# Softmax row sums partly added by accumulating DMAs, summed in a bank of the scores, and normalised on GpSimd

## The chip, the cores and the metric

One core of a Trainium2 chip runs one program. The metric is the device time of that program in microseconds (us), as the median of several runs. TensorE multiplies matrices, ScalarE applies functions such as the exponential, VectorE and GpSimd work on elements, SyncE issues most of the DMAs. SBUF holds 128 partitions of data; PSUM holds eight banks of 128 x 512 float32, into which TensorE writes.

## The reference, cut to what matters

The program computes attention with 32 heads of width 32 over 2 batches of 2048 rows, a gate made from a linear layer with a routed low-rank part, and their product added to the input.

```
xn     = layernorm(x)                                   # x: 2 x 2048 x 1024
q,k,v  = xn @ wq, xn @ wk, xn @ wv                      # 32 query heads, 8 key/value heads, width 32
scores = q k^T * 32**-0.5, causal mask
attn   = softmax(scores)                                # exp(s - shift) / row sum
s      = (attn @ v) @ wo
g      = silu(xn @ W_base.T + b + routed low-rank part)
out    = x + s * g
```

The change lies in the softmax: the sum of exp over the keys of each query row, and the division by it.

## The kernel before

The program has four parts, one after the other: `project` (layer norm, transposes, q, k, v and the low-rank part), `attend`, `gate` and `output`. The change is in `attend`, which works on 16 groups (2 batches x 8 key/value heads); each group has 4 query heads that share k and v.

Within a group the 2048 query rows are 4 chunks of 512 (c = 0 to 3). Chunk c needs key tiles j = 0 to 4c+3, of 128 keys each. For a pair of key tile j and query tile i, one matmul (L898) gives the scores of all four heads with the keys on the partitions, in one of 3 banks `cols_ps`; for tiles on the diagonal a second matmul (L901) adds the mask. ScalarE takes the exponential (L942) into `probs`, 5 buffers of 128 x 2048 that each hold one key tile j for the whole chunk. A group has 136 such tiles (10, 26, 42 and 58 by chunk), 2176 in all. The shift in the exponent comes from row maxima that are made ahead for the chunks to come: row scores (L818) into 3 banks `rows_ps`, then a maximum on VectorE (L963, or L967 with a mask). 84 of these row pieces are made before the group's first tile, and from there on about 1.2 per tile, so TensorE always alternates between L898 and L818.

The order of the work is written out by hand. `stage(c)` lists the operations: "T" a score tile, "S" a row piece, "M" the turning of the shifts, "W" the weighing of two key tiles, and the events of a finished chunk. All engines walk the same list and each carries out its own kinds, so an operation's place in the list sets what is queued behind it on its engine. `event(t, ...)` places an operation after tile t of the group.

"W" (function `weigh`) multiplies v with two `probs` tiles into `o_ps` (L856, four heads side by side; the trace has two records for each matmul, so 16 for two tiles). The row sums lie in their own bank `l_ps`: matmuls with a matrix of ones. Of the key tiles in `ADDS[c]` (L595: 0, 5, 8 and 11 of the tiles of the chunks) GpSimd makes one tile `added` (L801, one instruction for each but the first), and one set of matmuls sums that (L870); each other key tile has matmuls of its own (L863), in the same "W" as its L856.

When a chunk is done, "O" copies `l_ps` and `o_ps` to SBUF on ScalarE (L952, L953), and SyncE moves the sums: "L1" (L763) gathers them into a small tile, VectorE takes the reciprocal ("I", L1010), "L2" and "L3" (L767, L771) store it and spread it over the partitions, and "N" multiplies the chunk by it on VectorE (L1014, two inputs of 128 x 512 in SBUF). "L4" stores the chunk. The events stand 2, 4, 8, 9, 13, 18 and 19 tiles behind the chunk's last "W".

ScalarE writes key tile j into a buffer of `probs` only when the tile that was in it is weighed, and added where GpSimd adds it (L936 to L941).

```
1013:  dve.wait_ge(l_spread[cc % 2], n.lin(32 * NREP, 16 * NREP * (cc // 2 + 1) - 32 * NREP * back))
1014:  nc.vector.tensor_mul(o_sb[cc % 2][:, :], o_sb[cc % 2][:, :], l_all[cc % 2][:, :]).then_inc(norm_ready, 1)
```

Of the kernel before, what the change touches and what calls it, by code (L numbers as in the profile page):

```python
# [28 lines left out]
P = 128  # L29
B, S, D = 2, 2048, 1024  # L30
T = B * S
# [467 lines left out]
NROWS, NCOLS, NPROBS = 3, 3, 5  # L499
# [19 lines left out]
assert NJG % NPROBS == 0  # L519
# [7 lines left out]
def cols_slot(t):  # L527
    return 1 if t == NTG - 1 else t % NCOLS
# [16 lines left out]

EVENTS = {}
# [18 lines left out]

# [28 lines left out]

ADDS = [[], [0, 1, 2, 4, 5], [0, 1, 2, 4, 5, 6, 8, 9], [0, 1, 2, 4, 5, 6, 8, 9, 10, 12, 13]]  # L595
NADD = sum(len(a) - 1 for a in ADDS if a)


def adds_through(c, j):

    return sum(max(0, len(a) - 1) for a in ADDS[:c]) + sum(1 for t in ADDS[c][1:] if t <= j)


def attend(nc, sc, ident, ident_r, mask_ji, tri, wb, lb, gw_hi, gw_lo):

    ctx = ExitStack()
    with ctx:
# [13 lines left out]
        added = sb("added", [P, NREP, CH])  # L621
        row_max = [sb(f"row_max{i}", [P, NREP, TPC, CPB]) for i in range(2)]
# [7 lines left out]
        l_all = [sb(f"l_all{i}", [P, CH]) for i in range(2)]  # L630
        gw_raw = sb("gw_raw", [P, 2, D])
# [3 lines left out]
        l_ps = ctx.enter_context(nc.psum_tensor("l_ps", [P, CH], FP32))  # L635

        passed = sem("a_passed")
        passed_rows = sem("a_passed_rows")
        q_loaded = [sem(f"a_q_loaded{i}") for i in range(CPB)]
# [11 lines left out]
        sum_done = sem("a_sum_done")  # L651
# [36 lines left out]
        def probs_of(c, j):  # L688
            return probs[(J_OFF[c] + j) % NPROBS]
# [18 lines left out]
        def _(sp):  # L708
# [30 lines left out]
            def run(n, c, ops):  # L739
                last_group = isinstance(n.pair, int) and n.lin(1) == NG - 1  # L740
                for op in ops:
                    kind = op[0]
                    if kind == "T" and op[2:] == (0, 0):

                        if c > 0 or not isinstance(n.pair, int) or n.pair > 0 or n.u > 0:
                            wait_apart(sp, probs_ready, n.lin(NTG, T_OFF[c]), passed)
# [7 lines left out]
                    elif kind == "M":  # L754
                        move_row(rows_count(n, op[1], op[2]), op[4])
                    elif kind in ("L1", "L2", "L3", "L4"):
                        cc, back = op[1:3]
                        par = cc % 2
                        count = n.lin(CPB, cc + 1 - CPB * back)
                        few = sc["l_inv"][par].rearrange("h (x f) -> (h x) f", f=NL)  # L760
                        if kind == "L1":
                            wait_apart(sp, chunk_copied, count, passed)
                            sp.dma_start(l_few[par][:, :], l_sb[par][0:P:HD, :].rearrange("h (x f) -> h x f", f=NL)) \  # L763
                              .then_inc(l_moved[par], 16)
                        elif kind == "L2":
                            wait_apart(sp, l_inv_ready, count, passed)
                            sp.dma_start(few, l_inv[par][:, :]).then_inc(l_inv_stored, 16)  # L767
                        elif kind == "L3":
                            wait_apart(sp, l_inv_stored, n.lin(16 * CPB, 16 * (cc + 1 - CPB * back)), passed)
                            for h in range(NREP):  # L770
                                sp.dma_start(l_all[par][h * HD:(h + 1) * HD, :], sc["l_inv"][par, h, :].partition_broadcast(HD)) \  # L771
# [11 lines left out]
        def _(pool):  # L783
# [28 lines left out]
        def _(pe):  # L812
# [14 lines left out]
            pe.sem_inc(rows_full, 1)  # L827
            pe.wait_ge(ones_ready, 1)
# [12 lines left out]
            def weigh(n, cc, back, j0):  # L841

                steps = TPC * (cc + 1)
                to_sum = [j for j in range(steps) if j not in ADDS[cc]]
# [7 lines left out]
                pe.wait_ge(probs_ready, n.lin(NTG, tiles_through(cc, j0 + 1) - back * NTG))  # L852
# [6 lines left out]
                for j in (j0, j0 + 1):  # L859
                    q0 = max(0, j - TPC * cc) * P  # L860
                    if j in to_sum:
                        for h in range(NREP):
                            ins = nc.tensor.matmul(l_ps[h * HD:(h + 1) * HD, q0:CH], ones[:, :],  # L863
                                                   probs_of(cc, j)[:, h, q0:CH], start=(j == to_sum[0]),
                                                   stop=(j == to_sum[-1] and not ADDS[cc]), tile_position=(0, h * HD))
                ins.then_inc(values_done, 1)
                if j0 == steps - 2 and ADDS[cc]:
                    pe.wait_ge(pool_added, n.lin(NADD, adds_through(cc, NJG) - back * NADD))
                    for h in range(NREP):
                        ins = nc.tensor.matmul(l_ps[h * HD:(h + 1) * HD, :], ones[:, :], added[:, h, :],  # L870
                                               start=False, stop=True, tile_position=(0, h * HD))
                    ins.then_inc(sum_done, 1)

            def run(n, c, ops):
                for op in ops:
# [12 lines left out]
                    elif kind == "T":  # L888
# [14 lines left out]
                    elif kind == "W":  # L903
                        weigh(n, *op[1:])
            over_stages(pe, run)

        @block.scalar
        def _(act):
            def load_gw(k):
# [14 lines left out]
            def run(n, c, ops):  # L924
                first_group = isinstance(n.pair, int) and n.pair == 0 and n.u == 0
                for op in ops:
                    kind = op[0]
                    if kind == "T":
                        t, j, i = op[1:]
                        act.wait_ge(cols_full, n.lin(NTG, t + 1))  # L930
                        if i == max(0, j - TPC * c):

                            g = J_OFF[c] + j - NPROBS
                            back = 1 if g < 0 else 0
                            if not (back and first_group):
                                act.wait_ge(values_done, n.lin(NVG, g // 2 + 1))  # L936
                                c5 = CPB - 1 if back else max(cc for cc in range(CPB) if J_OFF[cc] <= g)
                                j5 = g + back * NJG - J_OFF[c5]
                                if j5 in ADDS[c5]:
                                    act.wait_ge(pool_added, n.lin(NADD, max(adds_through(c5, j5), adds_through(c5, ADDS[c5][1]))  # L940
                                                                  - back * NADD))  # L941
# [15 lines left out]
        def _(dve):  # L957
# [37 lines left out]
            def run(n, c, ops):  # L995
                for op in ops:
# [270 lines left out]
def program(nc, x, wall, wo, wb, b_base, lb, out):  # L1267
# [14 lines left out]
    with ExitStack() as ctx:  # L1282
        ident = ctx.enter_context(nc.sbuf_tensor("ident", [P, P], FP32))
        tri = ctx.enter_context(nc.sbuf_tensor("tri", [P, CH], FP32))
        plain_ji = ctx.enter_context(nc.sbuf_tensor("plain_ji", [P, NREP, P], FP32))
# [4 lines left out]
        with nc.Block() as block:  # L1290
# [51 lines left out]
```

## Time and profile before

| | |
|---|---|
| median of 3 runs | 3931.12 us (3921.78 to 3934.61) |
| the profiled execution's own time | 3927.28 us |
| its span, first to last instruction | 3925.5 us |
| mean granted TensorE clock | 0.938 |
| busy: TensorE 91%, VectorE 54%, GpSimd 39%, ScalarE 37% | of the span |

The attention part takes the stretch from about 735 to 3150 us. PE is a matmul and PEld a weight load of TensorE, DVE is VectorE, ACT ScalarE, POOL GpSimd, SPq SyncE's queue. A line number such as L898 is a line of the kernel before. PEclk is the clock that TensorE was granted, as a share of 2.4 GHz.

### The profile page before, as it was taken

Reading aid. Unit: us, or ns where it says so; the run is one execution under the profiler, and the core shown is the slowest. Engines: PE = TensorE matmul, PEld = TensorE weight load, DVE = VectorE, ACT = ScalarE, POOL = GpSimd, SP = SyncE. Lnnn points to the kernel's source line nnn. Section 1 sums busy time; section 2 is a strip of 40 time slices with the busy share of each in tenths; the row PEclk is TensorE's granted clock in tenths of the full one; section 3 lists DMA queues with packets and bytes.
Section 4 is the critical chain, followed back from the end, with each engine's and each line's share of the span. In section 5 each row is a group of like instructions: output and inputs, shape, how many; then the busy total and the mean of one; then the engine's idle time right before and its main releaser. Section 6 shows DMA issues by size and latency. Waiting matters only on the chain. (4 is left out here: it accounts for less than half of the span.)

```text
span 3925.5 us, 62611 instructions
## 1 busy us (share of the span) xinstructions
PE 3565.3 (91%) x19072; PEld 2261.0 (58%) x19072; DVE 2117.8 (54%) x4677; ACT 1466.8 (37%) x2658; POOL 1526.7 (39%) x366
## 2 busy tenths in 40 slices
PE   7999998998988888888988989888888879998999
PEld 6888886444444444444444444444444368887887
DVE  5333323766666666666667667666767322222333
ACT  3122111454555454554545545544545511110000
POOL 0000000566565575665665665655756700000000
PEclk9999998798998998998989999988999989999999
DMA  6555554211111102112112112112020044444555
GB/s 215 171 167 161 156 158 128 74 45 36 51 43 38 50 22 59 47 27 53 50 32 53 42 37 53 36 44 51 20 60 26 12 154 150 140 140 149 193 193 176
DMA packets 262851, 344.52 MB, mean 88 GB/s; under 512 B 38560, under 2 KB 154272, under 8 KB 261024
## 3 DMA queue, kind: packets, MB, share of 16 engines
q1 hardware_dynamic: 258960, 328.32, 27.8%
q10 hardware_dynamic: 3600, 12.58, 0.9%
q8 instruction: 150, 2.46, 0.3%
q14 instruction: 141, 1.16, 0.1%
HBM read 205.03 MB, written 134.74 MB: 87 GB/s over the span
## 5 line engine op out<-in xcount | busy, mean ns | idle before, releaser
L942 ACT ACTIVATE probs<-cols_ps 128x512 f32<-128x512 f32 x2176 | 1180.1, 607 | 1191.9 <-PE cols_ps L898 1075.4
L801 POOL TENSOR_TENSOR added<-added,probs 128x2048 f32<-128x2048 f32 (+1 forms) x288 | 1282.2, 4452 | 374.6 <-ACT probs L942 359.2
L818 PE MATMUL rows_ps<-k_st,q_st 96*128 96x512 f32 (+3 forms) x2560 | 1015.2, 419 | 247.1 <-DVE row_max L963 163.4
L963 DVE TENSOR_REDUCE row_max<-rows_ps 128x1 f32<-128x512 f32 x1536 | 1007.3, 685 | 415.8 <-PE rows_ps L818 411.3
L898 PE MATMUL cols_ps<-q_st,k_st 97*128 97x512 f32 x2176 | 943.8, 442 | 23.7 <-ACT probs L942 11.9
L818 PEld LDWEIGHTS rows_ps<-k_st,q_st 96*128 96x128 f32 x2560 | 515.8, 202 | 538.0 <-DVE row_max L963 343.3
L967 DVE CUSTOM_DVE_ANT_0 masked_rows<-rows_ps,tri 128x128 bf16<-128x128 f32 (+3 forms) x1024 | 488.4, 484 | 319.3 <-PE rows_ps L818 316.6
L898 PEld LDWEIGHTS cols_ps<-q_st,k_st 97*128 97x128 f32 x2176 | 431.3, 199 | 379.0 <-issue 258.2
L856 PE MATMUL o_ps<-probs,v_st 128*32 128x512 f32 (+3 forms) x5120 | 588.4, 581 | 1.1 <-ACT probs L942 1.1
L801 POOL TENSOR_TENSOR added<-probs 128x2048 f32<-128x2048 f32 x48 | 219.8, 4578 | 554.0 <-ACT probs L942 554.0
L856 PEld LDWEIGHTS o_ps<-probs,v_st 128*32 128x32 f32 x5120 | 142.4, 117 | 316.5 <-issue 252.7
L786 POOL TENSOR_TENSOR gw_lo<-gw_raw,gw_hi 128x1024 fp32r<-128x1024 f32 x9 | 21.2, 2360 | 687.6 <-ACT gw_hi L919 687.6
L438 PE MATMUL acc<-xt_hi,w_hi 128*128 128x512 f32 x704 | 281.6, 400 | 0.4 <-DVE logits L381 0.4
L440 PE MATMUL acc<-xt_hi,w_lo 128*128 128x512 f32 x704 | 277.6, 394 | 0.0
L439 PE MATMUL acc<-xt_lo,w_hi 128*128 128x512 f32 x704 | 276.8, 393 | 0.0
L1140 PE MATMUL g_acc<-gw_hi,g_t_hi 128*128 128x512 f32 x576 | 224.8, 390 | 19.7 <-DMA g_t_lo<-scratch_hw_lo 19.7
L395 DVE SCALAR_TENSOR_TENSOR out_lo<-acc,out_hi 128x512 fp32r<-128x512 f32 x80 | 55.3, 691 | 324.3 <-ACT out_hi L290 324.3
L1014 DVE TENSOR_TENSOR o_sb<-o_sb,l_all 128x512 f32<-128x512 f32 x64 | 221.8, 3466 | 10.9 <-DMA l_all<-scratch_l_inv 10.9
L1142 PE MATMUL g_acc<-gw_hi,g_t_lo 128*128 128x512 f32 x576 | 224.6, 390 | 0.0
L1141 PE MATMUL g_acc<-gw_lo,g_t_hi 128*128 128x512 f32 x576 | 224.5, 390 | 0.0
L1260 PE MATMUL o_acc<-ow_hi,o_t_hi 128*128 128x512 f32 x512 | 200.3, 391 | 11.2 <-DVE o_t_lo L1226 11.2
L1261 PE MATMUL o_acc<-ow_lo,o_t_hi 128*128 128x512 f32 x512 | 199.9, 391 | 0.0
(101 smaller groups left out, 3032.8 us busy)
## 6 DMA issues: line engine op xcount, KB each, us to landing
q_st<-scratch_q_hi SPq DMA_DIRECT2D x128, 256.0 KB, 4.5
x_sb<-in_x SPq DMA_DIRECT2D x32, 512.0 KB, 4.1
scratch_xt_hi<-xt_hi SPq DMA_DIRECT2D x32, 512.0 KB, 6.0
scratch_xt_lo<-xt_lo SPq DMA_DIRECT2D x32, 512.0 KB, 6.8
scratch_q_hi<-out_hi SPq DMA_DIRECT2D x64, 256.0 KB, 2.4
scratch_q_lo<-out_lo SPq DMA_DIRECT2D x64, 256.0 KB, 2.9
q_st<-scratch_q_lo SPq DMA_DIRECT2D x64, 256.0 KB, 4.6
l_all<-scratch_l_inv SPq DMA_DIRECT2D x256, 64.0 KB, 2.0
```

The source lines that it names most:

```text
L438: nc.tensor.matmul(out, lh, rh, start=(k == 0), stop=False)
L439: nc.tensor.matmul(out, lh, rl, start=False, stop=False)
L440: ins = nc.tensor.matmul(out, ll, rh, start=False, stop=(k == KT - 1))
L801: nc.gpsimd.tensor_tensor(added[:, :, q0:CH], other[:, :, q0:CH], probs_of(c, j)[:, :, q0:CH], ALU.add).then_inc(pool_added, 1)
L818: nc.tensor.matmul(rows_ps[rows_slot(k)][:, 0:keys], q_st[c][0:K1, h, i * P:(i + 1) * P], k_st[kbuf][0:K1, CH * p:CH * p + keys], start=Tr ...
L856: ins = nc.tensor.matmul(o_ps[h * HD:(h + 1) * HD, q0:CH], v_st[vbuf][:, j, :], probs_of(cc, j)[:, h, q0:CH], start=(j == 0), stop=(j == s ...
L898: ins = nc.tensor.matmul(into, k_st[n.u][:, j * P:(j + 1) * P], q_st[c][:, :, i * P:(i + 1) * P], start=True, stop=not diagonal)
L942: nc.scalar.activation(probs_of(c, j)[:, :, i * P:(i + 1) * P], cols_ps[cols_slot(t)][:, :].rearrange("p (h q) -> p h q", h=NREP), ACT.Exp) \
L963: nc.vector.tensor_reduce(into, bank[:, :], AX.X, ALU.max).then_inc(rows_free, 1)
L967: nc.vector.tensor_tensor_reduce(masked_rows[rows_slot(k)][:, 0:keys], bank[:, 0:keys], tri[:, CH - keys:CH], 1.0, MASKED, ALU.add, ALU.ma ...
L1140: nc.tensor.matmul(acc[half][:, :], t_hi[u][:, k, :], w_hi[:, k, cols], start=(k == 0), stop=False)
L1142: ins = nc.tensor.matmul(acc[half][:, :], t_lo[u][:, k, :], w_hi[:, k, cols], start=False, stop=(k == NW - 1))
```

## The change

Six key tiles fit instead of five (`NPROBS` 6), the row scores have four banks instead of three (`NROWS` 4), and the bank `l_ps` is gone. Of the key tiles of chunks 1 to 3, GpSimd adds 4, 6 and 9 (`ADDS`; 3, 5 and 8 instructions), and DMAs issued from GpSimd's queue add 2, 4 and 5 (`DMA_ADDS`): the first is a copy into `dma_added`, the others are SBUF to SBUF with accumulation. A new operation "Y" (`row_sums`) comes right behind the chunk's last "W": it sums `added`, `dma_added` and the key tiles that are left (two for chunks 1 to 3, four for chunk 0) with matmuls into one of the 3 banks `cols_ps`, which takes its turn among the score tiles. Before "Y" TensorE waits for the GpSimd adds and the DMA adds of the chunk. ScalarE copies that bank to SBUF before its next tile. GpSimd's operations are now placed in the list as events "A" (add), "D" (DMA add) and "N". "N" runs on GpSimd. The events I, L2, L3, N, L4 stand 11, 12, 15, 19 and 20 tiles behind. The buffer for the gate's weights shares memory with the sixth `probs` buffer.

```diff
-NROWS, NCOLS, NPROBS = 3, 3, 5
+NROWS, NCOLS, NPROBS = 4, 3, 6
+ADDS = [[], [0, 1, 2, 4], [0, 1, 3, 4, 6, 8], [0, 1, 3, 4, 6, 7, 9, 10, 12]]
+DMA_ADDS = [[], [3, 5], [2, 5, 7, 9], [2, 5, 8, 11, 13]]
+REST = [[j for j in range(TPC * (c + 1)) if j not in ADDS[c] + DMA_ADDS[c]] for c in range(CPB)]
+    event(_t, "Y", _c)
     event(_t + 2, "O", _c)
     event(_t + 4, "L1", _c)
-    event(_t + 8, "I", _c)
-    event(_t + 9, "L2", _c)
-    event(_t + 13, "L3", _c)
-    event(_t + 18, "N", _c)
-    event(_t + 19, "L4", _c)
+    event(_t + 11, "I", _c)
+    event(_t + 12, "L2", _c)
+    event(_t + 15, "L3", _c)
+    event(_t + 19, "N", _c)
+    event(_t + 20, "L4", _c)
+    for _j in ADDS[_c][1:]:
+        event(tiles_through(_c, _j) - 1, "A", _c, _j)
+    for _j in DMA_ADDS[_c]:
+        event(tiles_through(_c, _j) - 1, "D", _c, _j)
...
+            def dma_add(n, c, back, j):
+                q0 = max(0, j - TPC * c) * P
+                wait_apart(pool, probs_ready, n.lin(NUG, used_through(c, j)), passed_pool)
+                if j == DMA_ADDS[c][0]:
+                    if sum_before(n, c) is not None:
+                        wait_apart(pool, cols_full, sum_before(n, c), passed_pool)
+                    pool.dma_start(dma_added[:, :, :], probs_of(c, j)[:, :, :]).then_inc(dma_done, 16)
+                else:
+                    wait_apart(pool, dma_done, n.lin(16 * NDMA, 16 * (dma_adds_through(c, j) - 1)), passed_pool)
+                    pool.dma_start(dma_added[:, :, q0:CH], probs_of(c, j)[:, :, q0:CH], accum_op=ALU.add).then_inc(dma_done, 16)
...
+                    elif op[0] == "N":
+                        _, cc, back = op
+                        wait_apart(pool, chunk_copied, n.lin(CPB, cc + 1 - CPB * back), passed_pool)
+                        wait_apart(pool, l_spread[cc % 2], n.lin(32 * NREP, 16 * NREP * (cc // 2 + 1) - 32 * NREP * back), passed_pool)
+                        nc.gpsimd.tensor_tensor(o_sb[cc % 2][:, :], o_sb[cc % 2][:, :], l_sb[cc % 2][:, :], ALU.mult) \
+                            .then_inc(norm_ready, 1)
...
-                for j in (j0, j0 + 1):
-                    q0 = max(0, j - TPC * cc) * P
-                    if j in to_sum:
-                        for h in range(NREP):
-                            ins = nc.tensor.matmul(l_ps[h * HD:(h + 1) * HD, q0:CH], ones[:, :],
...
+            def row_sums(n, cc, back):
+
+                bank = cols_ps[cols_slot(AT_Y[cc])]
+                pe.wait_ge(probs_ready, cols_free_count(n, AT_Y[cc]))
+                parts = [(probs_of(cc, j), max(0, j - TPC * cc) * P) for j in REST[cc]]
+                if ADDS[cc]:
+                    pe.wait_ge(pool_added, n.lin(NADD, adds_through(cc, NJG) - back * NADD))
+                    pe.wait_ge(dma_done, n.lin(16 * NDMA, 16 * (dma_adds_through(cc, NJG) - back * NDMA)))
+                    parts = [(added, 0), (dma_added, 0)] + parts
...
+                    elif kind == "Y":
+                        cc, back = op[1:3]
+                        act.wait_ge(cols_full, cols_count(n, AT_Y[cc]))
+                        act.wait_ge(o_stored[cc % 2], n.lin(32, 16 * (cc // 2) + 16 - 32 * back))
+                        nc.scalar.activation(l_sb[cc % 2][:, :], cols_ps[cols_slot(AT_Y[cc])][:, :], ACT.Copy) \
+                            .then_inc(probs_ready, 1)
...
-                    elif kind == "N":
-                        cc, back = op[1:3]
-                        dve.wait_ge(l_spread[cc % 2], n.lin(32 * NREP, 16 * NREP * (cc // 2 + 1) - 32 * NREP * back))
-                        nc.vector.tensor_mul(o_sb[cc % 2][:, :], o_sb[cc % 2][:, :], l_all[cc % 2][:, :]).then_inc(norm_ready, 1)
```

## Rows read from the trace of the kernel before

**Rows 1.** Windows view: the three parts of the program; per engine busy us (instructions).

```profile
core 0: us, PE busy (x) PEld busy (x) DVE busy (x) ACT busy (x) POOL busy (x), PEclk, DMA share, GB/s
0.00:735.00 735.00, 687.57 (x3422) 563.28 (x3423) 290.83 (x708) 164.28 (x277) 29.72 (x32) 0.95 0.52 162
735.00:3150.00 2415.00, 2133.88 (x12387) 1082.69 (x12386) 1602.80 (x3673) 1220.50 (x2278) 1496.99 (x335) 0.92 0.16 41
3150.00:3926.00 776.00, 743.88 (x3264) 615.03 (x3264) 224.21 (x298) 81.99 (x104) 0.00 (x0) 0.98 0.49 164
```

**Rows 2.** Groups by line, 735 to 3150 us: busy us, mean ns | idle before.

```profile
L801 POOL TENSOR_TENSOR added<-added,probs 128x2048 f32<-128x2048 f32 (+1 forms) x288 | 1282.2, 4452 | 374.6 <-ACT probs L942 359.2
...
L818 PE MATMUL rows_ps<-k_st,q_st 96*128 96x512 f32 (+3 forms) x2451 | 962.5, 411 | 228.9 <-DVE row_max L963 163.2 <-DVE row_max L967 62.0
...
L1014 DVE TENSOR_TENSOR o_sb<-o_sb,l_all 128x512 f32<-128x512 f32 x63 | 221.2, 3510 | 5.9 <-DMA l_all<-scratch_l_inv 5.9
...
L870 PE MATMUL l_ps<-added,ones 128*32 128x512 f32 x384 | 54.8, 618 | 16.1 <-POOL added L801 16.0
```

**Rows 3.** Timeline around one "N": VectorE, TensorE and GpSimd (start, us).

```profile
1507.47 4.06 DVE L1014 TENSOR_TENSOR o_sb<-o_sb,l_all 128x512 f32<-128x512 f32 x1
1511.46 1.27 DVE L963 TENSOR_REDUCE row_max<-rows_ps 128x1 f32<-128x512 f32 x2
...
1507.94 0.28 PE L818 MATMUL rows_ps<-k_st,q_st 96*128 96x256 f32 x1
1512.19 0.79 PE L818 MATMUL rows_ps<-k_st,q_st 96*128 96x512 f32 x1 [3.97 <-DVE row_max L963]
...
1506.44 8.40 POOL L801 TENSOR_TENSOR added<-added,probs 128x2048 f32<-128x2048 f32 x2 [6.26 <-ACT probs L942]
```

**Rows 4.** Timeline, TensorE: the stalls at the other three "N" of a group.

```profile
1543.52 0.80 PE L818 MATMUL rows_ps<-k_st,q_st 96*128 96x512 f32 x1 [4.13 <-DVE row_max L963]
...
1588.65 0.60 PE L818 MATMUL rows_ps<-k_st,q_st 96*128 96x512 f32 x1 [3.86 <-DVE row_max L967]
...
1648.11 1.10 PE L818 MATMUL rows_ps<-k_st,q_st 96*128 96x512 f32 x2 [1.29 <-DVE row_max L963]
```

**Rows 5.** Timeline: the last "N" of the kernel, with GpSimd idle, and the store.

```profile
3155.07 0.69 DVE L1014 TENSOR_TENSOR o_sb<-o_sb,l_all 128x512 f32<-128x512 f32 x1 [5.01 <-DMA l_all<-scratch_l_inv]
3155.85 0.36 SPq L776 DMA_DIRECT2D scratch_o<-o_sb  x1
```

**Rows 6.** Windows view: in the stall of rows 3, behind it, and after that.

```profile
1506.00:1512.00 6.00, 2.22 (x11) 1.45 (x9) 6.00 (x6) 2.36 (x5) 5.48 (x2) 0.87 0.00 0
1512.00:1518.00 6.00, 5.81 (x23) 2.68 (x24) 3.10 (x7) 1.19 (x2) 2.84 (x1) 0.56 0.29 77
1518.00:1538.00 20.00, 19.63 (x128) 10.12 (x128) 13.94 (x32) 12.01 (x23) 9.38 (x3) 1.00 0.20 45
```

**Rows 7.** Timeline, end of a chunk 2: ScalarE, GpSimd, TensorE.

```profile
1558.06 4.10 ACT L942 ACTIVATE probs<-cols_ps 128x512 f32<-128x512 f32 x7 [2.32 <-PE cols_ps L898]
...
1558.81 8.15 POOL L801 TENSOR_TENSOR added<-added,probs 128x2048 f32<-128x2048 f32 x2 [3.77 <-ACT probs L942]
...
1565.65 0.83 PE L863 MATMUL l_ps<-probs,ones 128*32 128x256 f32 x16
1567.02 1.06 PE L870 MATMUL l_ps<-added,ones 128*32 128x512 f32 x8 [0.53 <-POOL added L801]
```

**Rows 8.** Timeline, end of a chunk 3: ScalarE, TensorE.

```profile
1617.30 1.57 ACT L942 ACTIVATE probs<-cols_ps 128x512 f32<-128x512 f32 x3 [0.25 <-PE cols_ps L901]
...
1625.72 1.06 PE L870 MATMUL l_ps<-added,ones 128*32 128x512 f32 x8
```

**Rows 9.** DMA issues: kind, engine, count, KB each, median us from issue to landing.

```profile
q_st<-row SPq DMA_DIRECT2D x64, 8.0 KB, 1.8
...
gw_raw<-in_wb ACTq DMA_DIRECT2D x8, 512.0 KB, 3.5
...
scratch_xt_hi<-xt_hi SPq DMA_DIRECT2D x32, 512.0 KB, 6.0
```

More of the change, by code:

```diff
@@ L556, with used_through @@
         event(_t, "W", _c, _j)
+    event(_t, "Y", _c)
     event(_t + 2, "O", _c)
     event(_t + 4, "L1", _c)
-    event(_t + 8, "I", _c)
-    event(_t + 9, "L2", _c)
-    event(_t + 13, "L3", _c)
-    event(_t + 18, "N", _c)
-    event(_t + 19, "L4", _c)
-event(VISIT_AFTER + 2, "K", 0)
+    event(_t + 11, "I", _c)
[7 more added lines that the diff above has]
+        event(tiles_through(_c, _j) - 1, "D", _c, _j)
+event(VISIT_AFTER + 2, "K", 0)
+COLS = []
+for _t in range(NTG):
+    COLS.append(("T", _t))
+    COLS += [("Y", e[1]) for e in EVENTS.get(_t, []) if e[0] == "Y"]
+NUG = len(COLS)
+AT_T = [COLS.index(("T", t)) for t in range(NTG)]
+AT_Y = [COLS.index(("Y", c)) for c in range(CPB)]
+def used_through(c, j):
+    return AT_T[tiles_through(c, j) - 1] + 1
 def stage(c):
@@ L621, in attend @@
         added = sb("added", [P, NREP, CH])
+        dma_added = sb("dma_added", [P, NREP, CH])
         row_max = [sb(f"row_max{i}", [P, NREP, TPC, CPB]) for i in range(2)]
@@ L629, in attend @@
         l_inv = [sb(f"l_inv{i}", [P, NL]) for i in range(2)]
-        l_all = [sb(f"l_all{i}", [P, CH]) for i in range(2)]
-        gw_raw = sb("gw_raw", [P, 2, D])
+        gw_raw = probs[NPROBS - 1][:, :, :].rearrange("p (a h) q -> p a (h q)", a=2)
         rows_ps = [ctx.enter_context(nc.psum_tensor(f"rows_ps{i}", [P, CH], FP32)) for i in range(NROWS)]
@@ L688, in probs_of, with first_group, cols_count, cols_free_count @@
         def probs_of(c, j):
-            return probs[(J_OFF[c] + j) % NPROBS]
+            return probs[probs_slot(J_OFF[c] + j)]
+        def first_group(n):
+            return isinstance(n.pair, int) and n.lin(1) == 0
+        def cols_count(n, u):
+            if first_group(n):
+                return u + 2 if u < AT_Y[CPB - 1] else u + 1
+            if isinstance(n.pair, int) and n.lin(1) == NG:
+                return n.lin(NUG, 1)
+            return n.lin(NUG, u + 1)
+        def cols_free_count(n, u):
+            if isinstance(n.pair, int) and n.lin(1) == NG:
+                return n.lin(NUG, 0)
+            before = before_in(cols_slot, NUG, u)
+            return None if first_group(n) and before < 0 else cols_count(n, before)
+        def sum_before(n, c):
+            if c == 1:
+                return None if first_group(n) else cols_count(n, AT_Y[CPB - 1])
+            return cols_count(n, AT_Y[c - 1])
         def rows_count(n, ahead, k):
@@ L843, in weigh @@
                 steps = TPC * (cc + 1)
-                to_sum = [j for j in range(steps) if j not in ADDS[cc]]
                 vbuf = (n.u + back) % 2
@@ L858, in weigh @@
                                                tile_position=(0, h * HD))
-                for j in (j0, j0 + 1):
-                    q0 = max(0, j - TPC * cc) * P
-                    if j in to_sum:
-                        for h in range(NREP):
-                            ins = nc.tensor.matmul(l_ps[h * HD:(h + 1) * HD, q0:CH], ones[:, :],
-                                                   probs_of(cc, j)[:, h, q0:CH], start=(j == to_sum[0]),
-                                                   stop=(j == to_sum[-1] and not ADDS[cc]), tile_position=(0, h * HD))
-                ins.then_inc(values_done, 1)
-                if j0 == steps - 2 and ADDS[cc]:
+                ins.then_inc(values_done, 1)
+            def row_sums(n, cc, back):
[3 more added lines that the diff above has]
+                if ADDS[cc]:
                     pe.wait_ge(pool_added, n.lin(NADD, adds_through(cc, NJG) - back * NADD))
+                    pe.wait_ge(dma_done, n.lin(16 * NDMA, 16 * (dma_adds_through(cc, NJG) - back * NDMA)))
+                    parts = [(added, 0), (dma_added, 0)] + parts
+                for k, (part, q0) in enumerate(parts):
                     for h in range(NREP):
-                        ins = nc.tensor.matmul(l_ps[h * HD:(h + 1) * HD, :], ones[:, :], added[:, h, :],
-                                               start=False, stop=True, tile_position=(0, h * HD))
-                    ins.then_inc(sum_done, 1)
+                        ins = nc.tensor.matmul(bank[h * HD:(h + 1) * HD, q0:CH], ones[:, :], part[:, h, q0:CH],
+                                               start=(k == 0), stop=(k == len(parts) - 1), tile_position=(0, h * HD))
+                ins.then_inc(cols_full, 1)
             def run(n, c, ops):
@@ L936, in run @@
                                 act.wait_ge(values_done, n.lin(NVG, g // 2 + 1))
[L937 to L940, printed above, removed]
+                                cb = CPB - 1 if back else max(cc for cc in range(CPB) if J_OFF[cc] <= g)
```

76 lines of the change are left out of this document (43 added, 33 removed).

## The prediction

> **What bounds the kernel now.** I read the windows view first: attention takes 2415 of the 3925.5 us, its TensorE is busy 2134 us and idle 281 us, and its clock averages 0.92, while the parts before and after are at 0.95 and 0.98 [rows 1]. No other engine is near: VectorE 1603, GpSimd 1497, ScalarE 1221 us. So TensorE sets the pace of this stretch, and there are two things to win beside its own work: its idle time and its clock. The groups by line then say where it idles: 228.9 us ahead of L818, the row scores, released by VectorE's maxima [rows 2]. The timeline shows how. At 1507.47 VectorE starts "N" (L1014), and it takes 4.06 us; the three banks of row scores fill, TensorE stops at 1508.2 and goes on at 1512.19, after 3.97 us of idle. GpSimd is inside an add that began at 1506.44 [rows 3]. The same multiplication took 0.69 us when GpSimd was idle [rows 5], so "N" itself is short; it is held until the GpSimd add ends, and the row maxima queue behind it on VectorE. The other three "N" of a group stop TensorE for 4.13, 3.86 and 1.29 us [rows 4]. This pattern repeats in all groups; 63 "N" fall in the stretch, mean 3510 ns [rows 2].
>
> The clock follows these stalls. In the 6 us with the stall it is 0.87 on average, in the 6 us behind it 0.56, mostly the lower level of 1.2 GHz, and in the 20 us after that 1.00 [rows 6].
>
> **The change, part by part.** The sum is made against the profiled execution, 3927.3 us, which is 3.8 us under the median of the three runs; I take it as that. Differences under 0.3% (12 us) can't be told from no change here.
>
> 1. "N" leaves VectorE. Per group 3.97 + 4.13 + 3.86 + 1.29 = 13.25 us of TensorE idle [rows 3, 4], for 15.5 groups (the last has no row scores behind its end): 205 us gone. On GpSimd "N" has a quarter of the elements of an add of 4.45 us [rows 2], so 1.1 us, 64 times. I cost that at nothing on TensorE but in chunk 1 (below), because GpSimd makes 5 adds fewer in each group: 16 x 4.45 + 4 x 1.1 = 76 us where it had 21 adds, 94 us. VectorE is left with no instruction that reads two tiles in SBUF while GpSimd works.
>
> 2. The clock. A mean of 0.92 over 2415 us means 2 x 0.08 x 2415 = 386 us at the lower level, 6.2 us for each of 62 stalls. Of those, 2 x 0.13 x 6 = 1.6 us lie in the stall [rows 6], where they cost nothing. The other 4.6 us do half the work: 2.3 us lost each, 143 us in all. They go with the stalls.
>
> 3. Row sum matmuls. Full key tiles summed by TensorE, the tile `added` among them, were 2, 3 and 4 in chunks 1 to 3 and are 2 in each: 3 fewer per group. One costs 54.8 us / 48 = 1.1 us [rows 2] (384 records, 8 for each). 3 x 16 x 1.1 = 53 us. The sums of the diagonal tiles and of chunk 0 stay, and only move to "Y".
>
> 4. The fourth bank. Of the 228.9 us ahead of L818 [rows 2], 205 are the stalls of step 1. Of the other 24 us I give 10 back. Bounds 0 and 24.
>
> 5. "Y" in a bank of the scores. It is one long item in the alternation of three banks, and ScalarE copies it before it can go on. The copy takes about 0.6 us, as an exponential does (7 in 4.10 us) [rows 7]; I take half of it as seen by TensorE, 0.3 x 64 = 20 us, bounds 0 and 38. The sixth buffer loosens ScalarE's waits for free buffers; these cost TensorE nearly nothing now, so 0. The gate's weights are in `probs` only until the first group's sixth key tile, 0.
>
> 6. The new wait, which decides the case. The last DMA add of a chunk takes the second key tile of the diagonal, j = 4c+1, and stands on GpSimd's queue behind the add of j = 4c. "Y" waits for it, with all of TensorE's work queued behind. Take as zero the end of the exponentials of j = 4c. GpSimd's add runs from 0.1 to 4.6. Then comes the issue, and then the transfer of 768 KB with accumulation. TensorE's time of arrival can be read: in chunk 2 the first of the seven exponentials ends at 1558.06 + 4.10 / 7 = 1558.7, GpSimd starts at 1558.81, and L870 starts at 1567.02 after a wait of 0.53, so TensorE came at 7.8 [rows 7]. The sums of 0.83 us ahead of it [rows 7] now come behind the wait: 7.0. In chunk 3 the three of the next key tile start at 1617.30 after 0.25 of idle, so zero is 1617.05; 1625.7 - 1617.1 = 8.6 [rows 8], less 0.8: 7.8. Chunk 1 I give 7.0.
>
> The price of such a DMA isn't in this trace. A plain one of 8 KB lands in 1.8 us, one of 512 KB in 3.5 [rows 9]: 3.4 ns a KB, so 4.4 us for 768 KB and 5.3 us for 1 MB if an accumulating DMA goes at the rate of a plain one. This is the lower end. The upper end: it must also read its destination, so twice the data, 7.0 and 8.8 us; stores of 512 KB that queue behind one another take 6.0 us [rows 9], so even plain ones can be at this end. I take the lower end, since the row nearest to it is a DMA that has the engines to itself, as this one mostly has (DMA share 0.16 [rows 1]). The issue on GpSimd I take as 1 us, between SyncE's 0.36 [rows 5] and 2.5, as an estimate.
>
> The Trainium skill, "DMA: Bandwidth & Descriptors", section "Anatomy of one DMA — SWDGE (gpsimd) path", fits a DMA from GpSimd's queue as 2.0 us plus its bytes over 436 GB/s. That estimate would be 3.8 us for 768 KB, 0.6 us less in each of 48 waits, and the sum 29 us lower; no run here shows it.
>
> With 4.4 us the DMA lands at 4.6 + 1 + 4.4 = 10.0. TensorE waits 3.0 us in chunk 2 and 2.2 in chunk 3. In chunk 1 the "N" of chunk 0 stands between the add of j = 4 and the DMA of j = 5, so 1.1 later: 4.1 us. 9.3 x 16 = 149 us. The earlier DMA adds, three key tiles apart (some 10 us), are then landed in time. Each of the 48 waits also costs the clock as the present stalls do, 2.3 us: 110 us. In return the present wait for GpSimd's adds, 16 us [rows 2], is contained in it.
>
> 7. The tail of the last group: 3 us for the later landing.
>
> Sum: 3927 - 205 - 143 - 53 - 10 = 3516; + 20 + 149 + 110 - 16 + 3 = 3782 us.
>
> **The rivals.**
>
> A. The accumulating DMA reads twice, 7.0 and 8.8 us. Then the one before it isn't landed either. In chunk 3 the DMA of j = 11 is issued at -0.6, after two adds back to back, and lands at 8.2; that of j = 13 follows at 9.2 and lands at 16.2, a wait of 8.4 us. In chunk 2 the same gives 15.3 and 8.3 us; in chunk 1 the first DMA is a copy, 13.7 and 6.7 us. 23.4 x 16 = 374 us, and the clock, with longer waits, some 2.8 us x 48 = 134 us: 3516 + 20 + 374 + 134 - 16 + 3 = 4031 us, slower. It decides from a mean wait of 6.1 us per chunk: 3523 + 110 + 48 x 6.1 = 3927. For it: the addition needs two streams. Against it: the DMA engines are idle by 84% here [rows 1].
>
> By the Trainium skill, "Collectives: The Full Stack", section "The bandwidth ceiling: the fold count and why AG ≠ RS ≠ AR", a reduction by DMA is slowed not by the addition but by its two source reads, and its rate is about half that of a copy. It speaks for A; no row here shows such a DMA.
>
> B. The waits are short, 1.3 us or less, as if the transfer took 2.5 us or TensorE came later because row scores hold it: 3523 + 48 x 1.3 = 3585 us if the clock then stays up, 3695 if it falls. For it: 256 KB less of each and full DMA engines. Against: the stall of 1.29 us is among those of today, and an 8 KB transfer alone takes 1.8 us [rows 9].
>
> C. VectorE becomes the bound. Without "N" it has (1603 - 221) / 2176 = 0.64 us a score tile, and TensorE after the change (2134 - 143 - 53) / 2176 = 0.89. On the mean it has room, but the row scores come in bursts between two "W". If steps 3 and 4 are lost to that: 3782 + 63 = 3845 us.
>
> **How the numbers follow.** The forecast, waits of 2 to 4.5 us per chunk: 0.5. A, slower: 0.25. B: 0.15. C: 0.1. The predicted time is that of the forecast, 3782 us. With issue and rate varied (each us of wait is 48 us) its own range is 3690 to 3880. The range over all cases goes from B's 3590 to A's 4035. Slower by over 0.3%: A, 0.25. Within 0.3%: 0.05, from waits near 6.1 us. Faster: the rest of the forecast, B and C, 0.70.
>
> **What would show it.** L818's idle should fall from 229 us to under 30. No two-input VectorE instruction should be longer than 1 us in attention. The clock's mean should be near 0.94: still below 1 because of the waits at "Y", and TensorE should idle 2 to 4.5 us ahead of the new sums in chunks 1 to 3, released by the DMA into `dma_added` and not by GpSimd. The last DMA add should land 4 to 5 us behind its issue; 7 or more would be A. GpSimd should show 4 "N" of about 1.1 us a group. The prediction is wrong if the idle before "Y" is under 1 us or over 6 us, or if L818 keeps waiting.

## The result, and the profile after

The changed kernel takes 4120.32 us (median of 4 runs, 4115.94 to 4128.13); the kernel before took 3929.98 beside it. The ratio is 1.049 [1.046 to 1.051]: slower by 4.9%, where 3782 us was forecast. The time lies above the range, and beyond rival A's 4031 us.

The windows view of the changed kernel, in the columns of [rows 1]:

```profile
0.00:735.00 735.00, 684.78 (x3422) 562.90 (x3423) 289.04 (x704) 163.60 (x276) 29.17 (x31) 0.95 0.51 162
735.00:3340.00 2605.00, 1969.55 (x12004) 1058.27 (x12002) 1359.47 (x3614) 1193.57 (x2279) 1403.72 (x496) 0.87 0.45 104
3340.00:4114.00 774.00, 745.38 (x3264) 616.29 (x3264) 223.45 (x296) 81.99 (x104) 0.93 (x1) 0.98 0.49 164
```

All of it is in attention, 2605 us in place of 2415. TensorE's busy time fell, by 164 us; its idle time rose from 281 to 635 us. The groups by line answer to [rows 2]:

```profile
L857 POOL TENSOR_TENSOR added<-added,probs 128x2048 f32<-128x2048 f32 x208 | 976.0, 4692 | 28.9 <-ACT probs L1026 21.2 <-POOL added L857 0.3
...
L892 PE MATMUL rows_ps<-k_st,q_st 96*128 96x512 f32 (+3 forms) x2452 | 852.6, 373 | 10.6 <-DVE row_max L1049 10.6
...
L946 PE MATMUL cols_ps<-added,ones 128*32 128x512 f32 x384 | 92.9, 1061 | 568.6 <-DMA dma_added<-probs 568.6
...
L881 POOL TENSOR_TENSOR o_sb<-o_sb,l_sb 128x512 f32<-128x512 f32 x64 | 82.0, 1282 | 102.8 <-DMA l_sb<-scratch_l_inv 102.8
```

The idle time ahead of the row scores is gone, 10.6 us for 228.9. In its place stand 568.6 us ahead of "Y" (L946 is `row_sums`), released by the DMA into `dma_added`, 48 times. GpSimd's "N" takes 1.28 us, but GpSimd also sat 102.8 us ahead of it. The timeline of one chunk 3, which answers to [rows 7, 8], ScalarE, then GpSimd, then TensorE:

```profile
1836.97 0.60 ACT L1026 ACTIVATE probs<-cols_ps 128x512 f32<-128x512 f32 x1 [1.88 <-PE cols_ps L973]
...
1829.84 9.59 POOL L857 TENSOR_TENSOR added<-added,probs 128x2048 f32<-128x2048 f32 x2
1839.37 0.85 POOL L869 DMA_DIRECT2D dma_added<-probs  x1
1839.98 4.87 POOL L857 TENSOR_TENSOR added<-added,probs 128x2048 f32<-128x2048 f32 x1
1848.19 1.31 POOL L869 DMA_DIRECT2D dma_added<-probs  x1 [3.35 <-DMA dma_added<-probs]
...
1844.32 0.86 PE L930 MATMUL o_ps<-probs,v_st 128*32 128x256 f32 x16
1858.86 1.93 PE L946 MATMUL cols_ps<-added,ones 128*32 128x512 f32 x8 [13.68 <-DMA dma_added<-probs]
```

Key tile 12 is done at 1837.6, the forecast's zero. TensorE comes to "Y" at 1845.2, so at 7.6 (forecast 7.8). But GpSimd is still in a pair of adds of key tiles 9 and 10, issues the DMA add of key tile 11 at 1.8 and not at -0.6, adds key tile 12 until 7.3, and then waits 3.35 us for the DMA of key tile 11. The last DMA add is issued at 10.6 (forecast 4.6) and lands at 21.2 (forecast 10.0). The DMA issues of the changed kernel, columns as in [rows 9]:

```profile
dma_added<-probs POOLq DMA_DIRECT2D x128, 1024.0 KB, 7.3
dma_added<-probs POOLq DMA_DIRECT2D x48, 768.0 KB, 9.2
q_st<-scratch_q_hi SPq DMA_DIRECT2D x128, 256.0 KB, 7.2
...
scratch_l_inv<-l_inv SPq DMA_DIRECT2D x64, 8.0 KB, 3.9
```

The small one of 768 KB lands later than the one of 1 MB. The first line mixes two kinds: the 48 plain copies (L866) have a median of 4.8 us, the 80 accumulating DMAs of 1 MB one of 7.7. The loads of q had taken 4.5 us, and the 8 KB store of the inverse sums 1.4.

### The profile page after: what moved, and what is told of

It is laid out like the page before. It is cut to its first block and busy times, and to the rows that moved or that the text cites. A ratio compares the mean times of both kernels' runs of the same rounds, so it can differ in the third digit from the quotient of the medians.

```text
span 4114.1 us, 62857 instructions
## 1 busy us (share of the span) xinstructions
PE 3399.7 (83%) x18688; PEld 2237.5 (54%) x18688; DVE 1872.0 (46%) x4613; ACT 1439.2 (35%) x2658; POOL 1433.8 (35%) x526
## 5 line engine op out<-in xcount | busy, mean ns | idle before, releaser
L1026 ACT ACTIVATE probs<-cols_ps 128x512 f32<-128x512 f32 x2176 | 1151.8, 611 | 583.8 <-PE cols_ps L973 494.9
L857 POOL TENSOR_TENSOR added<-added,probs 128x2048 f32<-128x2048 f32 x208 | 976.0, 4692 | 28.9 <-ACT probs L1026 21.2
L973 PE MATMUL cols_ps<-q_st,k_st 97*128 97x512 f32 x2176 | 912.3, 428 | 41.5 <-issue 31.5
L892 PE MATMUL rows_ps<-k_st,q_st 96*128 96x512 f32 (+3 forms) x2560 | 902.6, 382 | 28.2 <-DMA q_st<-scratch_q_hi 16.9
L973 PEld LDWEIGHTS cols_ps<-q_st,k_st 97*128 97x128 f32 x2176 | 414.9, 191 | 384.9 <-issue 244.3
L892 PEld LDWEIGHTS rows_ps<-k_st,q_st 96*128 96x128 f32 x2560 | 498.6, 195 | 168.6 <-DVE row_max L1049 72.0
L946 PE MATMUL cols_ps<-added,ones 128*32 128x512 f32 x384 | 92.9, 1061 | 568.6 <-DMA dma_added<-probs 568.6
L930 PE MATMUL o_ps<-probs,v_st 128*32 128x512 f32 (+3 forms) x5120 | 538.9, 539 | 0.0
L1033 ACT ACTIVATE l_sb<-cols_ps 128x512 f32<-128x512 f32 x64 | 38.2, 597 | 830.1 <-PE cols_ps L946 830.1
L946 PEld LDWEIGHTS cols_ps<-added,ones 128*32 128x32 f32 x384 | 9.8, 140 | 582.4 <-DMA dma_added<-probs 512.2
L842 POOL TENSOR_TENSOR gw_lo<-probs,gw_hi 128x1024 fp32r<-128x1024 f32 x9 | 21.2, 2363 | 687.8 <-ACT gw_hi L998 687.8
L1222 PE MATMUL g_acc<-gw_hi,g_t_hi 128*128 128x512 f32 x576 | 225.2, 391 | 21.2 <-DMA g_t_lo<-scratch_hw_lo 21.2
```

The source lines that it names most:

```text
L857: nc.gpsimd.tensor_tensor(added[:, :, q0:CH], other[:, :, q0:CH], probs_of(c, j)[:, :, q0:CH], ALU.add).then_inc(pool_added, 1)
L892: nc.tensor.matmul(rows_ps[rows_slot(k)][:, 0:keys], q_st[c][0:K1, h, i * P:(i + 1) * P], k_st[kbuf][0:K1, CH * p:CH * p + keys], start=Tr ...
L930: ins = nc.tensor.matmul(o_ps[h * HD:(h + 1) * HD, q0:CH], v_st[vbuf][:, j, :], probs_of(cc, j)[:, h, q0:CH], start=(j == 0), stop=(j == s ...
L973: ins = nc.tensor.matmul(into, k_st[n.u][:, j * P:(j + 1) * P], q_st[c][:, :, i * P:(i + 1) * P], start=True, stop=not diagonal)
L1222: nc.tensor.matmul(acc[half][:, :], t_hi[u][:, k, :], w_hi[:, k, cols], start=(k == 0), stop=False)
```

## The experiments

In all of them line numbers are those of the kernel in question. Times are medians of 4 runs; the kernel before took 3926 to 3931 us beside them. A line "..." in an edit stands for lines left out. "In the trace" means that the number is taken from all 16 groups of the run's trace and not from a line shown.

**e1, one part alone: "N" on GpSimd in the kernel before.**

```diff
-                        nc.vector.tensor_mul(o_sb[cc % 2][:, :], o_sb[cc % 2][:, :], l_all[cc % 2][:, :]).then_inc(norm_ready, 1)
...
+                        nc.gpsimd.tensor_tensor(o_sb[cc % 2][:, :], o_sb[cc % 2][:, :], l_all[cc % 2][:, :], ALU.mult) \
+                            .then_inc(norm_ready, 1)
...
```

So that "N" has a place among them, GpSimd's adds are put in the list as events too; they are the same 21 a group, in the same order.

> The kernel before, with the normalisation 'N' moved from VectorE to GpSimd and nothing else. Theory 1 (the stall at 'N' is VectorE held by a GpSimd add, and it costs 205 us of idle TensorE and 143 us of clock): 3930 - 348 = about 3580 us, the idle ahead of the row scores from 229 to under 30 us. Rival (the idle only moves: with 21 adds a group GpSimd becomes the bound and TensorE waits for `added`, or waits for row maxima elsewhere): over 3750 us.

3632.53 us, ratio 0.925 [0.923 to 0.926]: 293 us. The windows view of e1:

```profile
735.00:2855.00 2120.00, 2033.51 (x12389) 1030.43 (x12388) 1372.95 (x3612) 1218.56 (x2279) 1556.74 (x399) 0.98 0.18 47
```

That is 55 us less than the 348 expected, on the side of theory 1. Idle TensorE fell from 281 to 86 us, its busy time by 100 us with the clock at 0.98. So the reading of [rows 3 to 6] holds, with 100 us where 143 was given to the clock.

**e2, the last DMA add of each chunk to TensorE.**

```diff
-DMA_ADDS = [[], [3, 5], [2, 5, 7, 9], [2, 5, 8, 11, 13]]
+DMA_ADDS = [[], [3], [2, 5, 7], [2, 5, 8, 11]]
```

> The changed kernel, with the last DMA add of chunks 1 to 3 (key tile 4c+1) summed by TensorE in 'Y' instead. It adds 48 x 0.8 = 38 us of matmuls. Theory 1 (the 569 us of idle ahead of the sums are the landing of this last DMA, issued behind a GpSimd add): the idle falls to under 150 us, what is left being chunk 3, where the DMA before it lands late, and the time is 3620 to 3750 us. Rival (GpSimd is behind in any case, and any DMA add is late): over 3900 us.

3590.53 us, ratio 0.915 [0.913 to 0.916]; 530 us less than the changed kernel, though TensorE has more to do, and 30 us under the range expected. What is left at "Y" in e2's waits:

```profile
PE cols_ps L946 <- DMA dma_added<-probs: 85.4, 32, 6.4
```

**e3, no DMA add at all.**

```diff
-DMA_ADDS = [[], [3, 5], [2, 5, 7, 9], [2, 5, 8, 11, 13]]
+DMA_ADDS = [[], [], [], []]
+LEFT_OUT = [[], [3], [2, 5, 7], [2, 5, 8, 11]]
...
-                    parts = [(added, 0), (dma_added, 0)] + parts
+                    parts = [(added, 0)] + parts
```

> The changed kernel without any DMA add: key tile 4c+1 is summed by TensorE, and the key tiles 3 (chunk 1), 2, 5, 7 (chunk 2) and 2, 5, 8, 11 (chunk 3) are left out of the row sums altogether. It gives the time of everything else in the change. If the forecast's steps 1 to 5 hold (3523 us with no wait at all), then 3523 + 38 - 48 x 1.1 for the sums of the DMA tile that are gone = about 3510 us. If the other parts brought less than forecast: 3600 us or more.

3418.32 us, ratio 0.871 [0.869 to 0.872]. The rest of the change brings more than forecast, by 92 us. e10, in another variant, finds 53 of them: the fourth bank is worth 63 us where 10 were given. The others aren't traced.

**e4 and e9, "N" back on VectorE**, in the changed kernel and in e8 below.

```diff
-                    elif op[0] == "N":
...
+                    elif kind == "N":
+                        cc, back = op[1:3]
+                        wait_apart(dve, chunk_copied, n.lin(CPB, cc + 1 - CPB * back), passed_rows)
+                        dve.wait_ge(l_spread[cc % 2], n.lin(32 * NREP, 16 * NREP * (cc // 2 + 1) - 32 * NREP * back))
+                        nc.vector.tensor_mul(o_sb[cc % 2][:, :], o_sb[cc % 2][:, :], l_sb[cc % 2][:, :]).then_inc(norm_ready, 1)
```

> The changed kernel, with 'N' back on VectorE. Theory 1: the stalls at 'N' come back beside the waits at 'Y', 4 a group of 1.3 to 4 us and their clock: 4120 + 200 to 350, so 4320 to 4470 us. Rival (the waits at 'Y' give GpSimd and VectorE the time in which 'N' hides, so that moving it brought nothing here): within 60 us of 4120.

e4: 4120.84 us, so no difference at all, within what the rival had given. But the stalls are back, 177 us more of idle ahead of the row scores, TensorE is busy for 93 us more, and the wait at "Y" is 263 us smaller (e4's waits; L886 is the row scores, L940 is "Y"):

```profile
PE cols_ps L940 <- DMA dma_added<-probs: 305.5, 41, 13.2
PE rows_ps L886 <- DVE row_max L1043: 187.1, 105, 4.2
```

That could mean that "N" hides in the waits, or that it does harm which the waits at "Y" pay back. e9 was to decide:

> e8 with 'N' back on VectorE, so e4's edit where the DMAs no longer hold TensorE. Theory 1 (moving 'N' is worth its 200 us of stalls and their clock, and in e4 this was hidden because a TensorE that stalls at 'N' arrives that much later at 'Y' and waits less there for the DMA): 3546 + 200 to 350 us, so 3750 to 3900 us. Rival ('N' on VectorE is harmless beside four banks of row scores and fewer GpSimd adds): under 3620 us.

3796.36 us against e8's 3546.52: 250 us. So "N" on VectorE costs nearly the same as in e1 where TensorE sets the pace. Why it cost nothing in e4 shows when the attention part is cut from each "Y" to the next one (start to start, mean of the groups in the trace, us; e6 is described below and only takes chunk 0's "N" out of the way of the last DMA add of chunk 1):

| | to "Y" of chunk 0 | of chunk 1 | of chunk 2 | of chunk 3 |
|---|---|---|---|---|
| the changed kernel | 13.0 | 37.7 | 48.8 | 64.0 |
| e4, "N" on VectorE | 13.1 | 32.5 | 49.2 | 69.1 |
| e6 | 13.3 | 30.9 | 48.5 | 64.3 |

Two effects cancel, and that they are equal is luck. In chunk 1, e4 gains 5.2 us a group, since "N" no longer stands in GpSimd's queue ahead of the last DMA add; e6 gains 6.8 there by the same. In chunk 3, e4 loses 5.1 us. Only in chunk 2 does a stall of TensorE just shorten its wait at "Y": there the chain from the last "Y" over GpSimd's adds and DMAs sets the pace (the first add of a chunk waits for the last "Y", since `added` and `dma_added` have one buffer each).

**e5, the same DMAs without accumulation.**

```diff
-                    pool.dma_start(dma_added[:, :, q0:CH], probs_of(c, j)[:, :, q0:CH], accum_op=ALU.add).then_inc(dma_done, 16)
+                    pool.dma_start(dma_added[:, :, q0:CH], probs_of(c, j)[:, :, q0:CH]).then_inc(dma_done, 16)
```

> The changed kernel, whose DMAs into `dma_added` are all plain copies (nothing is accumulated, so part of the row sums is left out). Same instructions, sizes, queue and waits. Theory 1 (the accumulation makes a DMA land late by its reading of the destination: 1 MB accumulating 7.0 to 8.2 us, the plain one 4.6): all land in 4 to 5 us, the waits before 'Y' fall by 3 to 5 us each, and the time is 3850 to 3950 us. Rival (the wait is made of the queue in front of the DMA, GpSimd and its waits, and not of the transfer): over 4030 us.

3870.37 us, ratio 0.986 [0.984 to 0.988], 250 us less than the changed kernel. The DMA issues of e5:

```profile
dma_added<-probs POOLq DMA_DIRECT2D x128, 1024.0 KB, 4.7
dma_added<-probs POOLq DMA_DIRECT2D x48, 768.0 KB, 6.8
```

Its waits at "Y" sum to 313.7 us. Accumulating costs 255 us of the 568.6; 314 us are there with plain copies too. In chunks 2 and 3 much of this comes through the DMAs ahead of the last one: in the trace, the last DMA is issued 4.7 and 6.5 us behind the forecast's zero here (forecast 4.6), and 10.1 and 10.6 us in the changed kernel. In chunk 1 it is 12.4 us in both.

**e6, "N" of chunk 0 behind the last DMA add of chunk 1.**

```diff
-    event(_t + 19, "N", _c)
-    event(_t + 20, "L4", _c)
+    event(_t + (24 if _c == 0 else 19), "N", _c)
+    event(_t + (25 if _c == 0 else 20), "L4", _c)
```

> The changed kernel, with the 'N' and 'L4' of chunk 0 five tiles later, so that on GpSimd's queue 'N' stands behind the last DMA add of chunk 1 and not ahead of it. Theory 1 (in chunk 1 GpSimd waits about 5 us for the landing of the spread inverse sums, and the last DMA add behind it is late by that and by the 1.3 us of 'N'): the wait of chunk 1 falls from 14.5 to about 8 us, 16 x 6.5 = 100 us, so about 4020 us. Rival (the DMA add is late for its own reasons): within 30 us of 4120.

4008.55 us, ratio 1.020, 112 us less than the changed kernel, all of it in chunk 1 (table above); the waits at "Y" fell by 105 us. GpSimd's queue in a chunk 1 of the changed kernel shows what was moved:

```profile
1888.64 0.59 POOL L866 DMA_DIRECT2D dma_added<-probs  x1
1889.25 4.60 POOL L857 TENSOR_TENSOR added<-added,probs 128x2048 f32<-128x2048 f32 x1
1899.04 1.26 POOL L881 TENSOR_TENSOR o_sb<-o_sb,l_sb 128x512 f32<-128x512 f32 x1 [5.18 <-DMA l_sb<-scratch_l_inv]
1900.24 1.29 POOL L869 DMA_DIRECT2D dma_added<-probs  x1
```

The last DMA add could have gone out at 1893.9; it went at 1900.2. The spread of the inverse sums is itself held up: the 8 KB store ahead of it was issued at 1889.51, just behind the 1 MB copy of 1888.64, and the spread followed only at 1895.62. Without any DMA add (e3) this store takes 2.1 us in chunk 0, not 6.0 (medians in the trace), and GpSimd waits 59.3 us in all ahead of "N", not 102.8.

**e7, the loads of q (and k, v behind them) later.**

```diff
-                    if kind == "T" and op[2:] == (0, 0):
+                    if kind == "T" and op[2:] == (1, 1 if c == 0 else 0):
...
-                            wait_apart(sp, probs_ready, n.lin(NUG, AT_T[T_OFF[c] - 1] + 1 if c else 0), passed)
+                        wait_apart(sp, probs_ready, n.lin(NUG, AT_T[op[1] - 1] + 1), passed)
```

> The changed kernel, with the three loads of q at each chunk's start (and with them the loads of k and v behind them) issued a few tiles later, behind the wait at 'Y'. Theory 1 (the last DMA adds of chunks 1 and 3 share the DMA engines with these loads and land in 9.5 and 10.7 us where that of chunk 2 takes 6.3): they land in 6.3 to 7, the waits fall by 3 to 4 us in these chunks, and the time is about 4010 us. Rival (the landing is long for another reason, or the loads are then late for the row scores): over 4080 us.

3965.41 us, ratio 1.009 [1.008 to 1.011]: 155 us less than the changed kernel. The waits at "Y" fell by 137 us, to 431.1. In e7's DMA issues the 768 KB DMA now lands before the one of 1 MB:

```profile
dma_added<-probs POOLq DMA_DIRECT2D x128, 1024.0 KB, 6.9
dma_added<-probs POOLq DMA_DIRECT2D x48, 768.0 KB, 6.3
```

By chunk, the medians of the last DMA add in the trace were 9.5, 6.3 and 10.7 us in the changed kernel and are 6.4, 6.3 and 6.3 here. So 6.3 us is the price of 768 KB accumulated, and the rest was contention with the loads.

**e8 and e11, a faster version.** e8 also gives key tile 11 to TensorE; e11 adds e7's later loads.

```diff
-DMA_ADDS = [[], [3, 5], [2, 5, 7, 9], [2, 5, 8, 11, 13]]
+DMA_ADDS = [[], [3], [2, 5, 7], [2, 5, 8]]
```

> As e2 (the last DMA add of each chunk to TensorE), and in chunk 3 the add of key tile 11 as well. Theory 1: what is left of waiting in e2 is the DMA add of key tile 11, 2.4 us in each chunk 3, and the 2.0 us in chunk 2 for key tile 7; this adds 16 x 1.1 us of matmuls and takes away 16 x 2.4 us of waiting with some clock: 3590 - 20 to 30, about 3565 us. Rival (GpSimd's adds are as late as the DMA): 3590 to 3610 us.

> e8 with the loads of q later, as in e7. Theory 1 (e8 has no DMA add in flight at a chunk's start, so the place of the loads does nothing): 3546 within 15 us. Rival (the later loads cost, or clear the way for the sums' small DMAs): over 15 us either way.

e8: 3546.52 us, ratio 0.903 [0.902 to 0.905], a little better than expected, with 40.6 us of waiting at "Y". e11: 3513.74 us, ratio 0.894 [0.893 to 0.896]. The later loads brought 33 us where nothing was expected. Theory 1 was wrong in its premise: in e8 the DMA add of key tile 7 in chunk 2 is still in flight when TensorE comes to "Y". With the later loads its median falls from 8.1 to 6.9 us in the trace, and the wait of chunk 2 from 38 to 23 us in all. What the other 18 us are wasn't followed up. e11 leaves nothing of the computation out and is the fastest such kernel, 10.6% under the one before.

**e10, three banks for the row scores in e8.**

```diff
-NROWS, NCOLS, NPROBS = 4, 3, 6
+NROWS, NCOLS, NPROBS = 3, 3, 6
```

> e8 with three banks for row scores in place of four. Theory 1 (once 'N' is gone from VectorE, three banks run short by little): 3546 + 5 to 30 us. Rival (the row scores come in bursts between two 'W' that three banks don't carry): 3600 us or more.

3609.40 us: the fourth bank is worth 63 us, the rival's side. TensorE's idle time doesn't show it: 72 us in e10's attention part and 106 in e8's, while its busy time is 2028 and 1929 us. The weight loads ahead of the row scores do, e10 first, then e8:

```profile
L892 PEld LDWEIGHTS rows_ps<-k_st,q_st 96*128 96x128 f32 x2452 | 464.8, 190 | 331.8 <-DVE row_max L1049 214.0 <-DVE row_max L1053 66.3 <-issue 1.3
```

```profile
L892 PEld LDWEIGHTS rows_ps<-k_st,q_st 96*128 96x128 f32 x2449 | 465.2, 190 | 135.7 <-DVE row_max L1049 62.5 <-DVE row_max L1053 5.2 <-issue 0.2
```

Waits for VectorE of 280 us in sum become 68. Each is short (0.9 us at most with three banks) and counts as busy time of the matmuls, whose ends the profile models and does not measure.

**e12, key tile 4c+1 to GpSimd in e8.**

```diff
-ADDS = [[], [0, 1, 2, 4], [0, 1, 3, 4, 6, 8], [0, 1, 3, 4, 6, 7, 9, 10, 12]]
+ADDS = [[], [0, 1, 2, 4, 5], [0, 1, 3, 4, 6, 8, 9], [0, 1, 3, 4, 6, 7, 9, 10, 12, 13]]
```

> e8 with key tile 4c+1 of chunks 1 to 3 added by GpSimd, not summed by TensorE: 48 x 0.8 = 38 us of matmuls less. Theory 1 (GpSimd ends this add some 8 us after the key tile 4c is done and TensorE comes at 7 to 8, so it waits 0 to 2 us a chunk): 3510 to 3550 us. Rival (GpSimd, with 19 adds, 'N' and the DMA issues, falls behind, and TensorE waits for `added`): over 3580 us.

3729.54 us: the rival was right, by 183 us. TensorE waited 153.6 us for `added`. GpSimd's queue now ends behind TensorE. That isn't the number of adds alone: in e1 GpSimd makes 21 adds a group, those of key tile 4c+1 among them, and the "N", and TensorE waits 25.4 us for `added`. e1 has no DMA issues in that queue, and GpSimd waits 10.7 us ahead of "N" there, against 92.4 in e12; which of the two it is wasn't tested.

## Why the prediction was wrong, point by point

1. "N" off VectorE, 205 us of idle: right. The idle time ahead of the row scores fell by 218 us, and e1 and e9 price the whole of it, clock included, at 293 and 250 us where 348 were given.
2. The clock: right in kind; e1's busy time fell by 100 us, not 143. After a wait at "Y" it falls as it did after "N". The windows view of the changed kernel, in the wait of the chunk 3 above, behind it, and after that:

```profile
1845.00:1859.00 14.00, 0.32 (x12) 0.14 (x8) 0.32 (x2) 1.46 (x3) 1.31 (x1) 0.66 0.99 197
1859.00:1865.00 6.00, 6.00 (x39) 2.45 (x37) 0.77 (x2) 1.32 (x3) 0.00 (x0) 0.66 0.01 3
1865.00:1885.00 20.00, 19.89 (x140) 11.75 (x142) 15.43 (x38) 13.55 (x28) 6.72 (x2) 1.00 0.23 55
```

   Behind the wait, 2 x 0.34 x 6 = 4.1 us at 1.2 GHz cost 2.0 us, near the 2.3 of the forecast. The first line also shows the DMA engines 0.99 busy. In a wait of chunk 2, where the last DMA add of 768 KB is alone, they are 0.94 busy (1953.5 to 1958.3 us). The mean share of the part before the change, 0.16, had been taken as room; where the DMA adds meet other transfers there is none.
3. Row sum matmuls, 53 us less: there are 3 fewer per group as forecast, but their busy time in the attention part rose, from 254 to 289 us. The sums of `added` run right behind the wait, at the low clock: 1061 ns each, where they took 618. What the fewer matmuls are worth at one clock wasn't measured.
4. The fourth bank, 10 us with bounds 0 and 24: mis-sized, it is 63 us where it was measured (e10 against e8). The bound was read from TensorE's idle time, which leaves out waits of under a microsecond beneath running matmuls.
5. "Y" in a bank of the scores, 20 us, and the tail, 3 us: not measured alone. TensorE waits 5.0 us for ScalarE's exponentials in all of attention, so 20 us is rather too much.
6. The wait at "Y" is the step that failed: 149 us forecast, 568.6 measured. From the forecast's zero, the end of the exponentials of key tile 4c (medians over the groups in the trace, us; each pair is forecast, then measured):

| chunk | TensorE comes | last DMA add issued | it lands | mean wait |
|---|---|---|---|---|
| 1 | 7.0, 7.5 | 5.7, 12.4 | 11.1, 22.2 | 4.1, 11.6 |
| 2 | 7.0, 6.9 | 4.6, 10.1 | 10.0, 16.9 | 3.0, 10.1 |
| 3 | 7.8, 7.6 | 4.6, 10.6 | 10.0, 21.3 | 2.2, 13.8 |

   TensorE's arrival was right (in chunk 1 it comes at about 14.6 in 6 of the 16 groups, and the wait is 7 to 9 us there). The larger part of the error is the time of issue, 5.5 to 6.7 us late, and the smaller one the landing after it. Three things make them up:

   - The queue in front of the DMA. "N" was costed at its 1.1 us, not at the 5 us for which GpSimd waits ahead of it with the last DMA add of chunk 1 behind; 112 us (e6). In chunk 3 GpSimd was 2.4 us late for key tile 12 and then waited for the DMA of key tile 11. The forecast had taken the earlier DMA adds to be "landed in time"; GpSimd waited for one of them 30 times, 105.8 us in all.
   - The rate of an accumulating DMA. 768 KB take 6.3 us and 1 MB 7.3 (e7) to 7.7, where a plain 1 MB copy takes 4.7 to 4.8. From the start of the issue, the forecast had 1 + 4.4 = 5.4 us for the last DMA add, although its rows count from issue to landing and so hold the issue already; this extra 1 us made up for half of the low rate. So the rate hardly matters in the last DMA itself, but it does in those before it, which hold the queue. With plain copies (e5) the waits are 255 us less.
   - Contention. In chunks 1 and 3 the last DMA add meets the loads of q, k and v, which are issued at the same point of the list; 155 us (e7).

   These three amounts overlap and are not a sum.

Rival A had the chain right, a DMA add that the next one waits for, and gave 374 us of waiting. It fell short by contention and by "N". Its prices, 7.0 and 8.8 us, were above the measured 6.3 and 7.3 to 7.7; that the second stream is the reason for the price was not shown, only that accumulating costs more than copying.

The Trainium skill, "DMA: Bandwidth & Descriptors", section "Anatomy of one DMA — SWDGE (gpsimd) path", gives an estimate of 4.4 us for 1 MB by its fit, and the plain copies of 1 MB had medians of 4.7 (e5) and 4.8: there they agree. The accumulating DMAs are above it, with 7.3 us at the least contention (e7). The Trainium skill, "Collectives: The Full Stack", section "The bandwidth ceiling: the fold count and why AG ≠ RS ≠ AR", has a reduction in a ring at half the rate of a copy; here 1 MB took 7.3 us (e7) against 4.7, between the plain price and twice it.

## What to carry to other kernels

An asynchronous add that ends a chain has to be priced from its issue, and its issue from everything that the issuing queue waits for before it; here 314 of 569 us of waiting stayed with plain copies in its place, and dropping 3 of 11 such DMAs per group turned 4.9% slower into 8.5% faster. When a part that should help changes nothing (e4), repeat it where the other bound is gone (e9), and cut the time into stages: two effects of opposite sign can make one zero. And look for short waits in the weight loads, not in the matmuls' idle time.

## What the runs showed that was not expected

Small DMAs suffer from large ones: the 8 KB store of the inverse sums had a median of 1.4 us before and in e3, of 3.8 us beside plain 1 MB copies (e5) and of 3.9 beside accumulating ones. The loads of q went from 4.5 to 7.2 us; without the DMA adds they take 5.2 (e3), with plain copies 5.3 (e5), so these suffer from the accumulation. The issue of an accumulating DMA costs GpSimd 0.87 us for one row of 8 KB per partition and 1.3 us for four rows of 1.5 KB; a plain one costs 0.6 and 0.8 us (e5). And 16 GpSimd adds a group fit beside the DMAs in e8, while 19 cost 183 us (e12).
